# Zeros of two block-diagonal operands by transfer, and the last expert's product, weighing and store batch by batch

## What is computed

```python
x = x + attn(_layernorm(x))                 # 16 heads of 8; scores = -beta * hyperbolic distance, causal softmax
x = x + xattn(_layernorm(x), ctx, ctx)      # 4 heads of 32, gated linear attention (mLSTM), norm over each head
x = x + ffn(_layernorm(x))                  # 8 experts, top 2 of a softmax router
...
# xattn, what matters here: qk of each head of 32
qk = jnp.einsum('bhsd,bhtd->bhst', q, k) / jnp.sqrt(dh)
...
# ffn, what matters here
h = jax.nn.silu(g) * u
expert_out = jnp.einsum('nef,efd->ned', h, down_w) + down_b
y = jnp.einsum('ne,ned->nd', probs, expert_out)
```

## Time and profile before

| what | us |
|---|---|
| median of 3 runs | 283.74 |
| lowest and highest run | 280.57, 286.13 |
| profiled execution, device time | 281.8 |
| its span from the first to the last instruction | 279.8 |
| POOL busy in the span | 122.5 |
| DVE busy in the span | 210.7 |
| PE busy in the span | 211.4 |
| mean granted TensorE clock (of full) | 0.799 |

### The profile page before, as it was taken

How to read it: one execution, slowest core, us unless ns; L and a number is a source line. 1 busy time by engine, 2 the same in 40 slices (tenths; PEclk the granted TensorE clock), 3 DMA queues, 4 the chain that set the end, 5 groups by cost and what they waited for, 6 DMA issues and landing times. The chain is left out here.

```text
span 279.8 us, 4805 instructions
## 1 busy us (share of the span) xinstructions
PE 211.4 (76%) x1568; PEld 169.5 (61%) x1568; DVE 210.7 (75%) x509; ACT 166.7 (60%) x313; POOL 122.5 (44%) x154
## 2 busy tenths in 40 slices
PE   0785324887799778887899227998999399999992
PEld 0343223776677657775477126556988388889882
DVE  6777889999989999996575885733488964846552
ACT  2499899999888997972543212433464247623220
POOL 5331345677755776717266012002467526534000
PEclk9999755578656785575599755599999889999999
DMA  5408678880303286000000000000000000100001
GB/s 138 121 0 191 157 173 231 213 214 18 81 2 82 54 270 207 2 1 2 1 0 2 0 0 1 0 2 0 0 2 0 0 2 2 37 1 2 0 0 37
DMA packets 35528, 15.74 MB, mean 56 GB/s; under 512 B 18600, under 2 KB 33456, under 8 KB 35504
## 3 DMA queue, kind: packets, MB, share of 16 engines
q1 hardware_dynamic: 35504, 15.44, 21.2%
HBM read 10.46 MB, written 4.98 MB: 55 GB/s over the span
## 5 line engine op out<-in xcount | busy, mean ns | idle before, releaser
L815 ACT ACTIVATE dist_mem<-P,gub 128x512 f32<-128x512 f32 x32 | 21.9, 687 | 37.9 <-PE P L1185 37.9
L1156 DVE SCALAR_TENSOR_TENSOR dist_mem<-P,gub,dist_mem 128x512 f32<-128x512 f32 x32 | 23.7, 749 | 22.0 <-ACT dist_mem L815 21.9
L556 POOL TENSOR_SCALAR m_gt<-dist_mem 128x768 uint8<-128x768 f32 x16 | 34.3, 2144 | 6.7 <-issue 4.8
L1185 PE MATMUL P<-cf,dist 128*128 128x128 f32 x96 | 28.8, 386 | 7.4 <-ACT shift L751 7.4
L547 POOL TENSOR_TENSOR dist<-dist,cf 128x128 f32<-128x128 f32 x32 | 14.6, 456 | 40.9 <-DVE dist L1014 40.9
L1185 PE MATMUL PO<-proj_mem,dist_mem 128*128 128x128 f32 x256 | 31.4, 276 | 1.3 <-DVE ctx_sb L1167 1.3
L1185 PEld LDWEIGHTS PO<-proj_mem,dist_mem 128*128 128x128 f32 x256 | 30.7, 192 | 2.5 <-issue 1.5
L1185 PE MATMUL P<-xhi,whi 128*128 128x512 f32 x64 | 27.1, 423 | 6.1 <-DVE dist_mem L1156 5.6
L1185 PEld LDWEIGHTS P<-cf,dist 128*128 128x128 f32 x96 | 19.0, 198 | 13.7 <-ACT shift L751 10.0
L1185 PE MATMUL P<-shift,cb 128*128 128x128 bf16 x96 | 26.4, 286 | 0.0
L1185 PEld LDWEIGHTS PO<-vab,proj_mem 128*64 128x64 f32 x384 | 22.6, 178 | 5.7 <-ACT proj_mem L724 3.7
(11 more groups left out here) (217 smaller groups left out, 547.7 us busy)
## 6 DMA issues: line engine op xcount, KB each, us to landing
q_split<-split_mem SPq DMA_DIRECT2D x16, 128.0 KB, 2.6
k_split<-split_mem SPq DMA_DIRECT2D x4, 512.0 KB, 3.5
stq<-q_split SPq DMA_DIRECT2D x16, 128.0 KB
stk<-k_split SPq DMA_DIRECT2D x16, 128.0 KB
wgu<-gate_w SPq DMA_DIRECT2D x1, 1024.0 KB, 7.1
wgu<-up_w SPq DMA_DIRECT2D x1, 1024.0 KB, 9.6
x_sb<-x SPq DMA_DIRECT2D x2, 256.0 KB, 3.2
stn<-stack_init SPq DMA_DIRECT2D x2, 256.0 KB, 3.7
```

What stands on the lines that cost most here:

```text
L556: pool.tensor_scalar(m_gt[:, g.k % 2, :], e2[:, g.k % 2, :], 4.0 - ATT_EPS, None, ALU.is_gt).then_inc(sm["gt_done"], 1)
L815: A(sil[:, f, :], (P1, P2)[f][:, 0, :], ACT.Silu, bias=gub[:, 0, one:one + 1]).then_inc(sm["sil_done"], 1)
L1156: V.scalar_tensor_tensor(hT[:, z % 2 * 2 + f, :], (P1, P2)[f][:, 1, :], gub[:, 1, one:one + 1], sil[:, f, :], ALU.add, ALU.mult).then_inc( ...
L1185: return nc.tensor.matmul(out_, lhsT, rhs, start=start, stop=stop, **more)
```

## The change

The zeros: both memsets of POOL, and POOL's waits before them, are gone. A new DRAM input `no_rows` of 1 x 2048 zeros is read by two transfers that broadcast it to 128 partitions (1.05 MB written by each, 8 KB per partition). SP issues the first after the waits for the stored split operands, ahead of ctx and ctxT, and the second at the end of the loads, after a wait for the last transposes. `blocks(c)` waits for its transfer.

The end: for z = 15 alone, `down` writes batches 0 to 3 into the banks PM, P3 (two) and PO, signals after each batch, and waits for the weighing of z = 14 only before batch 3. `weigh` waits and signals batch by batch, and SP stores the second chunk in four transfers of 64 KB, each after the weighing of its batch.

```diff
+        xblk_mem = [split_mem[:, 0:CB * XH * S], dist_all[:, 0:CB * XH * S]]
+        xblk = [t.rearrange("p (b h s) -> p b h s", b=CB, h=XH) for t in xblk_mem]
...
+        def y_bank(z, b):
+
+            if z < 2 * E - 1:
+                return PO[:, b * D:(b + 1) * D]
+            return (PM[:, 0:D], P3[:, 0, 0:D], P3[:, 1, 0:D], PO[:, 0:D])[b]
...
             for n in range(2, NP):
                 sp.wait_ge(stored[n], 96)
+            sp.dma_start(xblk_mem[0], no_rows.to_broadcast([128, CB * XH * S])).then_inc(sm["xblk_zero"], 16)
             sp.dma_start(ctx_sb[:, :, :], ctx.rearrange("b s d -> s b d")).then_inc(sm["ctx_in"], 16)
...
             sp.dma_start(wd[:, :, :], down_w.rearrange("e (c f) d -> f (e c) d", c=FC)).then_inc(sm["exp_in"], 16)
-            for c in range(NCH):
-                sp.wait_ge(sm["added"] if c == 0 else sm["y_done"], E * (c + 1))
-                sp.dma_start(out.rearrange("b s d -> s b d")[:, c * CB:(c + 1) * CB, :],
-                             chunk(acc, c)).then_inc(sm["out_done"], 16)
-            sp.wait_ge(sm["out_done"], 16 * NCH)
+            sp.wait_ge(sm["t_full"], NU)
+            sp.dma_start(xblk_mem[1], no_rows.to_broadcast([128, CB * XH * S])).then_inc(sm["xblk_zero"], 16)
+            rows_out = out.rearrange("b s d -> s b d")
+            sp.wait_ge(sm["added"], E)
+            sp.dma_start(rows_out[:, 0:CB, :], chunk(acc, 0)).then_inc(sm["out_done"], 16)
+            for b in range(CB):
+                sp.wait_ge(sm["y_done"], 2 * E + b)
+                sp.dma_start(rows_out[:, CB + b:CB + b + 1, :], acc[:, CB + b:CB + b + 1, :]).then_inc(sm["out_done"], 16)
+            sp.wait_ge(sm["out_done"], 16 * (1 + CB))
...
-            def zeros(s):
-                if s == 5:
-                    for n in range(NP):
-
-                        if n == 0:
-                            pool.wait_ge(sm["q0_stored"], 64)
-                            pool.wait_ge(sm["k0_stored"], 16)
-                            pool.wait_ge(sm["n0_stored"], 16)
-                        else:
-                            pool.wait_ge(stored[n], 96)
-                    pool.memset(xblk[0][:, :, :, :], 0.0).then_inc(sm["xblk0"], 1)
-
             def blocks(c):
 
+                pool.wait_ge(sm["xblk_zero"], 16 * (c + 1))
                 pool.wait_ge(sm["xT_done"], NO[1, c] + 1)
...
                 prepare(z)
-                if z == 1:
-                    pool.wait_ge(sm["t_full"], NU)
-                    link(pool.memset(xblk[1][:, :, :, :], 0.0))
...
-                dve.wait_ge(sm["y_full"], z + 1)
+                final = z == 2 * E - 1
+                if not final:
+                    dve.wait_ge(sm["y_full"], z + 1)
...
                 for b in range(CB):
                     t = c * CB + b
-                    last = V.scalar_tensor_tensor(acc[:, t, :], PO[:, b * D:(b + 1) * D], wts[:, t, e:e + 1],
+                    if final:
+                        dve.wait_ge(sm["y_full"], z + 1 + b)
+                    last = V.scalar_tensor_tensor(acc[:, t, :], y_bank(z, b), wts[:, t, e:e + 1],
                                                   (x2 if e == 0 else acc)[:, t, :], ALU.mult, ALU.add)
-                last.then_inc(sm["y_done"], 1)
+                    if final:
+                        last.then_inc(sm["y_done"], 1)
+                if not final:
+                    last.then_inc(sm["y_done"], 1)
...
-                wait(pe, "y_done", z)
+                if z == 2 * E - 1:
+                    pe.wait_ge(sm["acc_done"], 2)
+                else:
+                    wait(pe, "y_done", z)
                 for b in range(CB):
+                    if z == 2 * E - 1 and b == CB - 1:
+                        pe.wait_ge(sm["y_done"], z)
                     for f in range(FC):
-                        last = mm(PO[:, b * D:(b + 1) * D], hT[:, z % 2 * 2 + f, b * S:(b + 1) * S], wd[:, z % E * FC + f, :],
+                        last = mm(y_bank(z, b), hT[:, z % 2 * 2 + f, b * S:(b + 1) * S], wd[:, z % E * FC + f, :],
                                   start=(f == 0), stop=(f == FC - 1))
-                last.then_inc(sm["y_full"], 1)
+                    if z == 2 * E - 1:
+                        last.then_inc(sm["y_full"], 1)
+                if z < 2 * E - 1:
+                    last.then_inc(sm["y_full"], 1)
```

More of the change, by code:

```diff
@@ L145, in decoder_layer @@
                   norm_scale, router_t, gate_w, gate_b, up_w, up_b, down_w, down_b,
-                  const_f, const_b, const_t, stack_init, out):
+                  const_f, const_b, const_t, stack_init, no_rows, out):
     fp32, bf16, fp32r = mybir.dt.float32, mybir.dt.bfloat16, mybir.dt.float32r
@@ L248, in decoder_layer @@
         oT = sb("oT", [128, 128])
-        xblk = [over(split_mem, [128, CB, XH, S]), over(dist_all, [128, CB, XH, S])]
+        xblk_mem = [split_mem[:, 0:CB * XH * S], dist_all[:, 0:CB * XH * S]]
+        xblk = [t.rearrange("p (b h s) -> p b h s", b=CB, h=XH) for t in xblk_mem]
         gpre = sb("gpre", [128, NCH, CB, 2 * XH])
@@ L301, in decoder_layer @@
                  "whi_done gu_full sil_done h_done y_full y_done added qk_full par_ln o_rec_done nm0_done nm1_done "
-                 "qk2_full hh_full hc_done hvar_done xhi_done wg_done xblk0 passed blk_done "
+                 "qk2_full hh_full hc_done hvar_done xhi_done wg_done xblk_zero passed blk_done "
                  "zeroed").split()
@@ L580, in _ @@
                 step(At(None, s))
-                zeros(s)
                 if s == 10:
@@ L1498 @@
         "const_f": const_f, "const_b": const_b, "const_t": const_t, "stack_init": stack_rows(),
+        "no_rows": np.zeros((1, CB * XH * S), np.float32),
     }
```

## The result

The changed kernel took 280.36 us in the median (276.74 to 285.52, 21 runs), the kernel before 283.74 us (279.69 to 288.69, 21 runs). The ratio is 0.9899, 95% interval 0.9856 to 0.9942: 2.9 us faster, between 1.6 and 4.1. The ratio takes of each kernel only the executions within 1.5% of its fastest, so it is not the ratio of the two medians (0.988). The forecast was 280.3.

A forecast was written before the change was run, and what follows sets the result against it. No engine was full over the span, so each edit was read in its stage: DVE paces the loop, the end is serial. 1.5 + 0 + 0 + 1.9 = 3.4 us off 283.74 gives 280.3, range 277.8 to 284.0.

The forecast's parts named there:

- the loop's share: Attention loop: removing POOL's first memset was to give 1.5 us, range 0.9 to 1.6.
- The end: Last microseconds: last expert's product, weighing and store by batch; DVE done 2.1 us earlier, tail gain 1.9 us (0.75 to 2.3).
- the landing of the last piece: Final store: a quarter of the bytes should land sooner than 2.3 us; 0.3 us counted.
- The hold: Attention loop: DVE's compare L1001, held by POOL's memset, falls from 2.17 to 0.55 us; 1.5 us taken as gain.
- The zero transfer: First 1.05 MB of zeros, queued by SP before context and stacks: 2.7 us at 386 GB/s, no net cost, range 0 to 8.
- Cost nothing: Attention loop: the next stack lands at 66, 2.3 us before PE needs it, so the first zeros delay nothing.
- about 2 us of the 2.7 reach its landing: SP's queue: the stack's issue overlapped the context load before, so its landing slips about 2 us, to 66.
- the rival of a starved PE: Attention loop: zeros ahead of the stacks make PE wait; at the bound 8 us slower, 288.3 us; chance 0.10.
- The second clearing: Turn from attention to expert products: memset replaced by a transfer issued at 150.1, landing before 167.12; net 0.
- The rival "only the tail": Whole kernel: the loop's 1.5 us are lost again in a later stage, only 1.9 us remain, 281.8 us; chance 0.20.
- The clock: Expert stage: TensorE's granted clock fall, some 1.5 us, removed or added by earlier arrival: 278.8 or 281.8; chance 0.14.

The follow-up runs named there:

- e9: The changed kernel measured once more with no edit, beside two later variants: 282.78 us, ratio 0.9895 to the kernel before.
- e2: The changed kernel with the last product, weighing and stores as before, so only both clearings go by transfer: 283.41 us, ratio 1.0001 to the kernel before.
- e3: The changed kernel with both clearings given back to POOL and the second chunk stored in one transfer: ratio 0.9993 to the kernel before.
- e4: The changed kernel with its first zero transfer moved behind all loads of stacks, ahead of the expert weights: ratio 0.9897 to the kernel before.

## Why the prediction held, and where it did not

- **The total.** 280.3 forecast, 280.36 measured. The sum was 3.4 us, the measured gain 2.9 with an interval of 1.6 to 4.1. The stretches give 2.2 us at the end and, by the means of the groups, 0.2 in the loop: 2.4, inside the interval. So the agreement rests on the end; the loop's share was smaller than forecast. That 280.36 falls within 0.1 us of 280.3 is luck: the measured gain is known to 1.3 us either way, and from 283.74 the ratio gives 280.9. The estimate at like clock, 3.7 us for this kernel and 2.4 for the same one as e9, allows a loop share from nothing to the forecast's 1.5.
- **The end.** The mechanism was right in each step: PE without a gap, DVE finished 2.2 us earlier in relation to the last `hidden` (5.53 before, 3.35 after; forecast 2.1), issues 0.45 us apart as taken. The term that was mis-sized is the landing of the last piece, 0.7 us shorter instead of 0.3: 2.2 us, not 1.9. That the split of the store brings nothing was not asked in the prediction. A slip of its sum: 12 instructions of 0.122 us from 272.57 end at 274.03, not 274.05, which changes nothing.
- **The hold.** The compare takes 0.55 us, and at the higher clock the step is 5.65 us, both as forecast; over three steps 1.5 to 1.6 us come back where the clocks are alike. What failed is that this was taken for every execution. The comparable step of the earlier trace rows had a fast product with v; in six of the ten executions without a memset there that product ran at the lower clock, and DVE waited for it. There the step is 6.11 to 6.14 us at best, so that about 1.2 of the 1.6 us come back. I had named ACT as what could take DVE's place.
- **The zero transfer.** "Cost nothing" held in two of four executions; in the others PE waited 0.55 and 0.53 us for the stack, and the group's mean loop is 0.6 us longer than without the transfer. The rate was right, against 386 GB/s assumed: 342 to 360 together with the context loads, 426 over a stretch of the second zero transfer, alone in the queue, and 4.7 us to its landing. Reading one DRAM row 128 times is no slower than the context rows. The failed step is "about 2 us of the 2.7 reach its landing". SP's two issues of `stq` and two of `stk` took 5.31 and 4.09 us instead of 1.26 and 1.65, so the last piece went out 5.9 us later in this execution (at 64.9 to 67.4 in the four with one early transfer, at 61.4 to 63.5 in those without, 3.5 us apart in the mean), and PE could start on the stack at 70.53, not at the 66 forecast. I had moved the bytes in the queue but kept the issue times of before. This is the rival of a starved PE, at a fraction of its price.
- **The second clearing.** Right: from the last closing copy to the first copy of `blocks(1)` it is 26.10 us before and 26.17 after.
- **The rival "only the tail"** came nearest: what is left of the loop's gain is 0.2 us by the means, and e2 at 1.0001 (up to 1.7 us either way) cannot tell it from nothing. But it had named a loss in a later stage, and what was seen is in the same one. How much of the loop's gain the changed kernel keeps on the mean stays open: the traces are too few for it and the medians too wide.
- **The clock** was priced at 1.5 us; single lumps of 1.9 and 4.8 us were seen, see below.

## What to carry to other kernels

A transfer is not free because its bytes fit a gap: look at who issues behind it on the same queue, and whether the issue itself takes longer while much is queued; put a load that is needed late behind those needed soon. A POOL operation next to a DVE one costs what the DVE instruction it meets loses, once DVE is the engine that the step waits for. Where a bank or a wait makes the last stage serial, breaking up the product and its evacuation pays (2.2 us here); breaking up the store did not. Before a gain of 1% is read from whole times, compare the granted clocks of the two sets of executions.

## What the runs showed of the hardware

SP's issue of a small transfer is not a fixed cost. With the 1.05 MB of the context loads issued just before, the two issues of `stq` took 1.26 to 2.17 us; with 1.05 MB of zeros more, 2.58 to 5.31; with 2.1 MB more, 5.83. The two of `stk` behind them took 1.23 to 3.82 us without early zeros and 3.66 to 4.09 with one transfer of them.

TensorE's granted clock made lumps larger than the effect studied. Stretches of the expert part's start, columns as in the earlier trace rows, of the kernel before and then of the changed one:

```profile
185.00:190.00 5.00, 5.00 (x28) 3.56 (x27) 2.27 (x4) 2.42 (x5) 0.00 (x0) 1.00 0.00 0
190.00:195.00 5.00, 3.86 (x22) 3.26 (x21) 1.61 (x3) 1.37 (x2) 1.87 (x2) 1.00 0.00 0
```

```profile
185.00:190.00 5.00, 5.00 (x19) 2.93 (x17) 1.38 (x2) 2.19 (x5) 0.00 (x0) 0.63 0.00 0
190.00:195.00 5.00, 5.00 (x15) 4.13 (x16) 0.89 (x2) 0.93 (x2) 0.00 (x0) 0.50 0.00 0
```

From the first copy of `blocks(1)` to the first `hidden` it took 25.3 to 25.6 us in eleven of the fourteen traces, 27.0 in e3, and 30.1 in the changed kernel's and in e4's, in which PE worked at the lower of its two levels (1.2 GHz) for several microseconds more. Likewise the step from unit 12 to unit 13 took 9.6 to 9.8 us in six traces and 11.5 in eight, among them kernels with and without each edit. The changed kernel's trace and e9's, the same program, differ by 6.6 us in these two stretches, and the runs of one kernel spread by 9 us: a gain of 1 us is not to be found in the medians here, only in stretches.
